# An adaptive feed-forward kernel: y's token rows by sixteen PE transposes, the first shared gate ahead of the rank products, warm-up products in three groups

## The reference

```python
x0 = x                                         # (32, 32, 256)
w = cond_weights[itok]                         # one 32x32 matrix per batch
y = einsum('bct,bcd->bdt', x, w)               # the conditioned tokens
xt = y.reshape(1024, 256)
probs = softmax(xt @ w_router)                 # 16 experts
top_w, top_i = top_k(probs, 4); top_w /= sum(top_w)
g = silu(xt @ we1[e]) * (xt @ we3[e]) * cw     # cw: the weight of expert e for a token, mostly 0
moe = sum over e of g @ we2[e]
shared = silu(xt @ ws1) * (xt @ ws3) @ ws2     # hidden width 512
out = x0 + shared / 5 + moe * 4 / 5
```

## Time and profile before

| | us |
|---|---|
| median of 3 runs | 148.45 |
| all runs | 146.96, 148.45, 149.17 |
| profiled execution | 146.87 |
| its span in the profile | 145.0 |
| PE busy | 133.6 (92% of the span) |
| DVE busy | 103.3 (71%) |
| ACT busy | 78.9 (54%) |

### The profile page before, as it was taken

One profiled execution on the slowest core, in us unless ns is written; L12 is line 12 of the kernel. 1 busy time (PEld: TensorE's weight loads), 2 busy tenths in 40 slices (PEclk: granted clock), 3 DMA queues, 4 the chain that ended last, 5 costly groups with the idle time before them and its releaser, 6 DMA issues.

```text
span 145.0 us, 2785 instructions
## 1 busy us (share of the span) xinstructions
PE 133.6 (92%) x786; PEld 112.0 (77%) x786; DVE 103.3 (71%) x290; ACT 78.9 (54%) x193; POOL 66.3 (46%) x79
## 2 busy tenths in 40 slices
PE   5999999989798999999999999899999999999470
PEld 2347997778487788999898889798999888888350
DVE  1301879998828999877879887887888653066992
ACT  4003637999404986677586777447945321107900
POOL 0700000002765687778776566577777777000000
PEclk9999999999999999999999999999999999999998
DMA  2823898989952232365437322122222222399924
GB/s 43 288 60 80 239 255 291 341 250 285 368 189 75 77 98 83 112 183 181 152 107 204 124 101 92 66 113 109 109 106 87 101 109 112 85 392 411 374 77 145
DMA packets 17549, 24.18 MB, mean 167 GB/s; under 512 B 3424, under 2 KB 14304, under 8 KB 17408
## 3 DMA queue, kind: packets, MB, share of 16 engines
q1 hardware_dynamic: 13440, 14.23, 30.1%
q0 software_dynamic: 3120, 8.52, 16.6%
q10 hardware_dynamic: 976, 1.26, 2.6%
HBM read 17.58 MB, written 6.42 MB: 166 GB/s over the span
## 4 chain that ended last, share of the span: by engine, by line
PE 61%; DVE 21%; DMA 7%; issue 5%; ACT 3%; DVEq 1%; ACTq 0%
PE up_ps L1004 17%; PE down_ps L1022 11%; PE down_ps L920 8%; PE gate_ps L907 5%; PE up_ps L907 4%; PE up_ps L998 4%; PE gate_ps L957 4%; PE down_ps L982 3%; PE down_ps L862 2%; DMA itok_rows<-in_itok_B 2%; DMA g<-in_L_cond_weights,cond_idx 2%; DVE g L632 2%; ACT w_hi L468 2%; DVE raw L805 2%; DVE x_lo L764 2%
## 5 line engine op out<-in xcount | busy, mean ns | idle before, releaser
L444 POOL DMA_INDIRECT result<-store_t,back_i x32 | 31.3, 979 | 12.9 <-issue 6.7
L437 POOL DMA_INDIRECT xt<-y_of,token_i x16 | 16.3, 1019 | 35.0 <-DVE token_i L716 28.1
L798 DVE SCALAR_TENSOR_TENSOR store_t<-down_ps,valid,store_t 128x256 f32 x47 | 21.7, 461 | 8.7 <-DVE store_t L798 5.8
L1004 PE MATMUL up_ps<-w_hi,x_hi 128*128 x78 | 23.8, 305 | 1.1 <-DVE x_lo L764 0.9
L1022 PE MATMUL down_ps<-w,gt 128*128 x94 | 24.5, 381 | 0.0
L1004 PE MATMUL up_ps<-w_lo,x_hi 128*128 x78 | 22.1, 283 | 0.0
L1004 PE MATMUL up_ps<-w_hi,x_lo 128*128 x78 | 22.0, 282 | 0.0
L437 POOL DMA_INDIRECT raw<-y_of,token_i x16 | 15.8, 985 | 4.9 <-issue 4.0
L1022 PEld LDWEIGHTS down_ps<-w,gt 128*128 128x128 f32 x94 | 16.0, 190 | 1.7 <-issue 0.5
L1004 PEld LDWEIGHTS up_ps<-w_hi,x_hi 128*128 128x128 f32 x78 | 14.8, 190 | 2.5 <-issue 2.4
L764 DVE TENSOR_TENSOR x_lo<-store_t,x_hi 128x256 fp32r<-128x256 f32 x39 | 14.8, 421 | 0.6 <-ACT x_hi L536 0.3
(11 more groups left out here) (156 smaller groups left out, 260.0 us busy)
## 6 DMA issues: line engine op xcount, KB each, us to landing
raw<-in_L_ffn_we SPq DMA_DIRECT2D x30, 128.0 KB, 3.3
w<-in_L_ffn_we SPq DMA_DIRECT2D x4, 512.0 KB, 6.4
w_lo<-result SPq DMA_DIRECT2D x4, 512.0 KB, 6.7
raw<-result SPq DMA_DIRECT2D x4, 512.0 KB, 7.0
acc<-in_x SPq DMA_DIRECT2D x2, 512.0 KB, 4.6
y_of<-store_t ACTq DMA_DIRECT2D x1, 1024.0 KB, 6.0
out<-acc SPq DMA_DIRECT2D x3, 256.0 KB, 2.2
xt<-in_L_ffn_ws SPq DMA_DIRECT2D x4, 128.0 KB, 2.7
```

The source lines that it names most:

```text
L437: pool.indirect_dma_start(rows_of(p)[:, j % 2, :], None, y_of, bass.IndirectOffsetOnAxis(ap=token_i[:, j:j + 1], axis=0),).then_inc(tile_i ...
L444: pool.indirect_dma_start(result, bass.IndirectOffsetOnAxis(ap=back_i[:, j:j + 1], axis=0), merged[:, j, :], None,).then_inc(result_out[j ...
L798: dve.scalar_tensor_tensor(out=into, in0=out_ps[n % 2][:, h, :], scalar=valid[:, it:it + 1], in1=into, op0=ALU.mult, op1=ALU.add).then_inc ...
L1004: last = pe.matmul(gu_ps[b][:, h, :], (x_hi, x_lo)[a][:, b, h, k * P:(k + 1) * P], pair_of(w, experts[h], k), start=(m == 0), stop=(m == 3 ...
```

## The change

The warm-up has 9 + 4 + 5 products of 128x256 instead of 8 of 128x512; the second group waits for `gathered`, the third for `cond_kept`. ACT makes a full float32 copy `y_f` of y transposed, bank by bank, ahead of `high(0)` and of `high(1)`. `token_rows` turns 128x128 blocks of `y_f` by PE transposes (16 of them), where it computed rows by 8 products of 128x256. ACT's copy of the rows no longer permutes columns. The small `Exp` for the top weights moves behind the DMA of the rows. On PE `gate_up(0, 0)` stands ahead of `ranks`.

```diff
-    WARM = 8
+    WARM = [9, 4, 5]
+        y_f = store_t[:, 0:TT, :].rearrange("p t d -> p (t d)").rearrange("p (k n) -> p k n", k=KD)
@@ scalar
-            high(0)
-            high(1)
+            for h in range(2):
+                for k in range(KD):
+                    act.wait_ge(y_lo_done, KD * h + k + 1)
+                    act.activation(y_f[:, k, h * HALF:(h + 1) * HALF], y_ps[h][k][:, :], ACT.Copy).then_inc(y_f_done, 1)
+                high(h)
             for j in range(4):
-                if j == 1:
-                    act.wait_ge(diff_done, 1)
-                    act.activation(top_e[:, :, :], top_d[:, :, :], ACT.Exp).then_inc(exp_done, 1)
                 act.wait_ge(row_done, j + 1)
-                act.activation(y_row[:, 2 * j:2 * j + 2, :].rearrange("p i (k c) -> p i k c", k=KD),
-                               row_ps[j][:, :].rearrange("p (i c k) -> p i k c", i=2, k=KD), ACT.Copy).then_inc(row_out, 1)
+                act.activation(y_row[:, 2 * j:2 * j + 2, :], row_ps[j][:, :].rearrange("p (i d) -> p i d", i=2), ACT.Copy).then_inc(row_out, 1)
             act.wait_ge(row_out, 4)
             act.dma_start(y_of.rearrange("(p t) d -> p t d", t=TT), y_row).then_inc(y_kept, 16)
+            act.wait_ge(diff_done, 1)
+            act.activation(top_e[:, :, :], top_d[:, :, :], ACT.Exp).then_inc(exp_done, 1)
@@ tensor
-            for i in range(WARM):
-                pe.matmul(row_ps[0][:, :], warm[:, 0:P], warm, start=True, stop=True)
+            def warm_up(n):
+                for _ in range(n):
+                    pe.matmul(row_ps[0][:, 0:D], warm[:, 0:P], warm[:, 0:D], start=True, stop=True)
+            warm_up(WARM[0])
+            pe.wait_ge(gathered, 16)
+            warm_up(WARM[1])
+            pe.wait_ge(cond_kept, 16)
+            warm_up(WARM[2])
             pe.wait_ge(cond_in, 16 * Q)
@@ token_rows(j)
+                if j % 2 == 0:
+                    pe.wait_ge(y_f_done, KD * (j // 2 + 1))
                 for i in range(2):
-                    last = pe.matmul(row_ps[j][:, i * D:(i + 1) * D], cond_bd[:, 2 * j + i, :], acc[:, 2 * j + i, :], start=True, stop=True)
+                    t = 2 * j + i
+                    for k in range(KD):
+                        last = pe.transpose(row_ps[j][:, i * D + k * P:i * D + (k + 1) * P], y_f[:, k, t * P:(t + 1) * P], ident[:, :])
                 last.then_inc(row_done, 1)
+            pe.wait_ge(const_done, 9)
@@
+            pe.wait_ge(dve_lo, 1)
+            gate_up(0, 0)
             ranks()
-            for s in range(2):
-                pe.wait_ge(dve_lo, 1)
-                if s == 1:
-                    pe.wait_ge(row_out, 4)
-                gate_up(s, 0)
-                gate_up(s, 1)
+            gate_up(0, 1)
+            pe.wait_ge(row_out, 4)
+            gate_up(1, 0)
+            gate_up(1, 1)
```

More of the change, by code:

```diff
@@ L223, in adaln_ffn @@
         row_out = sem("row_out")
+        y_f_done = sem("y_f_done")
         y_kept = sem("y_kept")
```

## The result

| | before | changed |
|---|---|---|
| median, 22 runs each | 148.45 | 148.66 |
| lowest, highest | 146.96, 151.94 | 148.11, 151.56 |
| mean | 148.64 | 149.01 |
| profiled execution, its span | 146.87, 145.0 | 149.95, 147.9 |
| ratio, 95% interval | | 1.0072, 1.0040 to 1.0105 |

By the ratio the change made the kernel a little slower; 2% is far off. The ratio leaves out executions more than 1.5% above the fastest of their kernel, which takes a level of 150.2 us away from the kernel before and leaves one of 149.9 us in for the changed one. By the medians of all 22 runs it is 1.0014, and with a standard deviation of 1.5 and 0.9 us the 0.4 us between the means of all runs are within the spread. The size of the loss is therefore not firm; what is firm is which times occur.

What follows compares the result with a forecast made beforehand. The bounding chain was taken as DMA, then PE, then DVE alone until g lets PE resume at 29.53 us. Warm-up +0.45 us and other terms 0 gave 147.3 (profiled) or 148.9 (median); it took 148.2, range 146.2 to 150.3.

Steps and rivals of the forecast that it cites:

- three signs: Wrong if: products behind `down(0)` at 0.4 us or more, counts over 0.8 us behind `mask`, y-to-`down(0)` distance moved over 0.3 us.
- The middle of two levels: Last step of the sum: between 147.3 us (profiled execution) and 148.9 us (median), it took 148.2 us.
- Rows by transposes, gate ahead of ranks: PE behind the logits: 16 transposes at 0.11 us end at 20.9, the gate at 22.3, `ranks` not held: 0.
- The clock's rival: Clock falls in PE's 1.95 us idle ahead of `down(0)`, costing 2.85 us: 150.2 or 151.8 us; 7 in 100.
- Transposes at the price of a pass: Rival: row transposes take 0.22 us each, `ranks` 1.25 us late, +1.2 us: 148.5 or 150.1 us; 8 in 100.
- Copies to y_f: ACT's copies ahead of `high(0)` delay DVE's first reduction by 0.90 us, into a slack of 0.92 us: 0.
- Warm-up: Start of PE's work: two extra old passes start y at 12.27 instead of 11.74 us; taken as +0.45 us.
- PE's time into the idle, ACT behind the rows: PE's saved 1.39 us falls into the idle ahead of `down(0)`; ACT's earlier work waits for DVE: 0 each.
- The faster rivals: PE's saved time reaches the end, 144.1 or 145.7 us, 6 in 100; warm-up change helps, about 147.0 us, 14 in 100.

Runs made afterwards that it cites:

- e7: The changed kernel with the logits' products four times as wide; median 147.86 us (12 runs).
- e3: The changed kernel with the ranks ahead of the first gate again; median 147.50 us (12 runs).
- e11: The kernel before, unaltered, run once more for a second trace; this execution took 150.16 us.
- e8: The kernel before with the first shared gate ahead of the ranks and nothing else; median 151.61 us (6 runs).
- e15: e7 again, unaltered, for a trace; this execution took 148.98 us.
- e16: e7 again, unaltered, for another trace; this execution took 148.61 us.
- e14: The changed kernel again, unaltered, for a trace; this execution took 148.92 us.
- e10: The changed kernel again, unaltered, for a trace; this execution took 149.83 us.
- e4: The changed kernel with the warm-up of the kernel before; median 148.24 us (12 runs).
- e13: The changed kernel again, unaltered, for a trace; this execution took 149.76 us.
- e5: e2 with the logits' products four times as wide; median 147.11 us (6 runs).
- e9: e7 with six unused products of 128x512 put into PE's idle ahead of `down(0)`; median 147.40 us (12 runs).
- e2: The kernel before with the copies to `y_f`, the rows by transposes and ACT's new order, old warm-up, ranks first; median 147.31 us (12 runs).
- e6: The kernel before with the logits' products four times as wide and nothing else; median 147.07 us (6 runs).

## Why the prediction was wrong

It forecast 148.2 (146.2 to 150.3), below the median of before. 148.66 lies in the range, but by the ratio (1.0040 to 1.0105) the kernel got slower. Two of the three signs that were to show an error showed it: the distance from y's first product to `down(0)` is 20.5 us instead of 17.8, and the counts are read 2.8 us behind the mask.

- **The middle of two levels.** The sum said +0.45 us, which is 148.9 from the median of before. I then took a mean of a low single execution and the median and landed below the kernel before. No row stood behind that step. The three times shown for before (146.96, 148.45, 149.17) already held the levels, and I called their spread unexplained instead of asking which of them the trace was.
- **Rows by transposes, gate ahead of ranks.** "6 products at the pace of 0.23 us are 1.39 us ... `ranks` isn't held, with 0.4 us to spare." This is the step that failed, a term put at 0. It holds at 2.4 GHz (e7's trace, counts at 23.41). In all four traces of the changed kernel the clock fell to 1.2 GHz at this place: the gate takes 1.8 to 2.4 us behind transposes of 3.0 to 3.5, and the counts come 1.1 to 2.8 us late. Undoing this one edit (e3) gives 147.50. It isn't the whole of the difference to the kernel before, whose rows are held up by the same falls (counts at 26.54 in e11); there the transposes give back a little more than the gate takes (26.14), and the kernel is slower because it has no run at 147, which stays open. That 148.66 lies in the range is luck: the range reaches there by rivals with other causes.
- **The clock's rival.** I gave 7 in 100 to a fall in PE's new idle. It is real: seen in the traces of e8, e15 and e16, and by time and clock likely in five of 12 runs of e7; in the changed kernel itself no trace has it. The idle was as forecast (1.95, measured 1.93 to 1.96). My reason against it, the idle of 1.83 us near the end that left the clock up, came from one execution; in e14 the idle at the same place, 2.03 us, was followed by a fall, and in e10 one of 2.06 us was not. The price was 1.7 us instead of 2.85, as the clock was back 3 to 4 us later and not after the 5.7 us that I had read at the start (5.9 by the clock record, which has the rise at 7.4 us and not at 7.2).
- **Transposes at the price of a pass.** By the profiled execution it happened, 0.22 us each, but from the clock and not from the operation. The counts came at 24.4 to 24.5 in e4, e13 and e14, the figure of this rival, by another cause. The Trainium skill's 275 ns for a bf16 transpose ("TensorE: Matmul & The Clock Gate", Part 4) is bettered by both paces of the float32 transposes here, 0.11 and 0.22 us each in a stream.
- **Copies to y_f.** Right: `low(0)` at 18.00 (forecast 17.95), the reduction at 18.61 (18.55), nothing on the chain. At the upper clock it is so too: e5 reads the counts at 23.35 (before 23.33).
- **Warm-up.** The working was right for its execution, with the late rise (e3, by its timeline: y starts at 12.33; forecast 12.27). It is one case of several: y starts at 11.8 in the first trace and at 12.45 in e9. In the medians the groups are worth -0.05 to 0.4 us.
- **PE's time into the idle, ACT behind the rows.** Right: `down(0)` waits for g in every trace, ACT waited 2.0 us for DVE's L678 (forecast 1.5).
- **The faster rivals** didn't occur. The gain that exists, 1.2 us of the transposes at the lower clock (e2), was in none of them.

## What to carry to other kernels

Where the times of a kernel have levels, find out which one the trace shows before pricing anything by it. The granted clock beside each time tells that the clock was down and for how long, not where; for that take a trace of each level. Price each edit ahead of a critical wait at both levels of TensorE's clock; an instruction moved into a slack of 0.4 us at 2.4 GHz was 1.1 to 2.8 us too much at 1.2 here. Ask also whether a level went away, not only whether a median moved. A pure reordering that hands PE's time to an idle is no gain and can be a loss, since PE may be at half pace behind the idle.

## What the runs showed of the hardware that I had not expected

- TensorE's clock fell to 1.2 GHz at about 18.6 us while PE had work in every microsecond from 14 to 18 us: y's products and the logits' 32-column products, each with a full weight load. With the same products four times as wide (0.05 us more in all) none of six runs of e6 was above 147.21 us, where 16 of 17 runs of the kernel before beside them were above 148.4.
- Behind an idle of 1.93 to 1.96 us the clock stayed up in six traces (changed, e4, e7, e10, e13, e14) and fell 0.2 to 1.1 us after PE took up work in three (e8, e15, e16). The three are those in which it had risen at 6.35 us or later.
- PE was busy all through the low stretches, from 18.6 to 25.4 us in the changed kernel and from 19.6 to 23.0 in e14, which is the same program.
